# Moving the block quantizer of a second FFN from GpSimd and VectorE to VectorE alone

## The reference

```python
def fake_quant_nvfp4(x, global_scale):          # blocks of 16
    amax = max(abs(xb))                         # per block
    sc8 = clip(amax / 6 * global_scale, 0, 448).astype(float8_e4m3fn)
    dq = sc8 / global_scale
    a = clip(abs(xb) / dq, 0, 6)
    q = sign(xb) * nearest(a, [0, .5, 1, 1.5, 2, 3, 4, 6])
    return q * dq
gate, up = quant(x) @ quant(gate_w).T, quant(x) @ quant(up_w).T
return quant(silu(gate) * up) @ quant(down_w).T
x = x + ffn(layernorm(x))
```

## Time and profile before

| | |
|---|---|
| runs | 979.66, 979.79, 981.98 us |
| median | 979.79 us |
| span of the profiled execution | 977.3 us (the profiler gives no time of its own for it beside the span) |
| busy: PE, DVE, ACT, POOL | 614.2, 629.9, 342.3, 329.3 us |
| mean granted clock of TensorE | 0.784 of full speed |

### The profile page before, as it was taken

One profiled execution on the slowest core, in us unless ns is written; L12 is line 12 of the kernel. 1 busy time (PEld: TensorE's weight loads), 2 busy tenths in 40 slices (PEclk: granted clock), 3 DMA queues, 4 the chain that ended last, 5 costly groups with the idle time before them and its releaser, 6 DMA issues.

```text
span 977.3 us, 19947 instructions
## 1 busy us (share of the span) xinstructions
PE 614.2 (63%) x5798; PEld 435.2 (45%) x5804; DVE 629.9 (64%) x2044; ACT 342.3 (35%) x797; POOL 329.3 (34%) x560
## 2 busy tenths in 40 slices
PE   5699999878886899922122227999981276722331
PEld 3588888754444666601010015777750154511110
DVE  2576767637773788778888865666646523267774
ACT  2255555522221465521111112444430134422332
POOL 2112111145553222146656553222100123255441
PEclk9799999979996899965555556999995569955555
DMA  8422232200001344200000012322300135300001
GB/s 247 93 64 58 60 71 56 50 8 1 0 0 33 90 98 97 66 9 0 0 0 0 0 26 64 82 70 64 73 15 0 33 107 136 105 1 0 0 0 43
DMA packets 99780, 46.96 MB, mean 48 GB/s; under 512 B 82992, under 2 KB 92272, under 8 KB 99696
## 3 DMA queue, kind: packets, MB, share of 16 engines
q1 hardware_dynamic: 99728, 46.34, 19.3%
HBM read 26.39 MB, written 19.92 MB: 47 GB/s over the span
## 4 chain that ended last, share of the span: by engine, by line
PE 36%; issue 22%; DVE 13%; POOLq 11%; POOL 10%; DVEq 4%; ACT 2%; DMA 1%; SPq 0%; ACTq 0%
PE bank L463 3%; POOL stats L994 3%; PE bank L430 2%; PE bank L492 2%; PE bank L435 2%; PE bank L446 2%; PE bank L414 2%; POOLq L1050 2%; POOLq L1052 2%; POOL small L1072 2%; PE bank L424 2%; POOLq L1055 2%; POOL att_t L1059 2%; PE bank L565 2%; PE bank L487 1%
## 5 line engine op out<-in xcount | busy, mean ns | idle before, releaser
L994 POOL TENSOR_TENSOR stats<-stats,half_neg 128x1 f32<-128x1 f32 x112 | 63.3, 565 | 251.1 <-DVE stats L1283 243.8
L808 ACT ACTIVATE probs<-bank 128x512 f32<-128x512 f32 x160 | 95.2, 597 | 88.3 <-PE bank L435 87.6
L1310 DVE TENSOR_REDUCE mx<-bank 128x4 f32<-128x512 f32 x160 | 108.1, 680 | 9.7 <-PE bank L414 9.1
L430 PE MATMUL bank<-q_stack,k_stack 128*128 128x128 bf16 x512 | 72.6, 222 | 1.5 <-DVE shift_t L1344 1.4
L435 PE MATMUL bank<-shift_t,sel_bf 128*128 128x128 bf16 x512 | 72.2, 221 | 0.0
L657 PE MATMUL bank<-ident_bf,probs 128*128 128x128 bf16 x16 | 4.6, 286 | 105.5 <-POOL probs L1053 105.5
L1021 POOL CAST q_parts<-resid 128x128 bf16<-128x128 f32 x48 | 14.4, 300 | 149.5 <-DVE resid L1325 149.5
L1288 DVE TENSOR_SCALAR xn<-x_sb,stats 128x128 f32 (+1 forms) x96 | 37.3, 389 | 35.4 <-POOL stats L994 35.1
L1325 DVE SCALAR_TENSOR_TENSOR resid<-bank,w_bias_cols,q_parts 128x128 f32<-128x128 f32 x48 | 16.8, 350 | 64.6 <-ACT q_parts L854 63.9
L1294 DVE TENSOR_TENSOR x_sb<-bank,x_sb 128x128 f32 (+1 forms) x64 | 18.5, 289 | 61.9 <-PE bank L570 26.6
L430 PEld LDWEIGHTS bank<-q_stack,k_stack 128*128 128x128 bf16 x512 | 50.1, 99 | 7.4 <-issue 5.8
(11 more groups left out here) (272 smaller groups left out, 1845.5 us busy)
## 6 DMA issues: line engine op xcount, KB each, us to landing
k_stack<-scratch_k SPq DMA_DIRECT2D x48, 192.0 KB, 3.4
q_stack<-scratch_q SPq DMA_DIRECT2D x48, 192.0 KB, 3.2
scratch_k<-k_parts SPq DMA_DIRECT2D x48, 96.0 KB, 1.8
scratch_q<-q_parts SPq DMA_DIRECT2D x48, 96.0 KB, 1.8
scratch_k<-k_parts SPq DMA_DIRECT2D x48, 64.0 KB, 1.6
scratch_q<-q_parts SPq DMA_DIRECT2D x48, 64.0 KB, 1.8
scratch_k<-k_parts SPq DMA_DIRECT2D x48, 32.0 KB, 1.5
scratch_q<-q_parts SPq DMA_DIRECT2D x48, 32.0 KB, 1.6
```

The source lines that it names most:

```text
L430: last = mm(o, k_stack[:, s, h, :], q_stack[:, s, h, :], start=layer == 1, stop=False, skip_group_check=True)
L808: activation(probs[:, (sP * U + u) % 4, :], bank[2 + u % 2][:, :], ACT.Tanh if layer == 3 else ACT.Exp, scale=float(d) ** -0.5).then_inc(s ...
L994: tt(stats[:, s, 9:10], stats[:, s, 8:9], half_neg[:, :], ALU.pow).then_inc(ln_rstd, 1)
L1310: reduce(mx[:, sM, u * UNIT:(u + 1) * UNIT], bank[u % 2][:, :].rearrange("p (h k) -> p h k", h=UNIT), AX.X, ALU.max).then_inc(sm["mx"], 1)
```

## The change

The wide instructions that GpSimd had in this FFN are removed there and a new function `fp4_blocks` does the whole quantization on VectorE, in the same step that computes the block scales. The order within it: product with the reciprocal scales; exponent mask, taken from the upper 16 bits of each 32-bit word (`[:, 1::2]` of a 16-bit view) into a 16-bit tile `magic4`; max and multiply on that 16-bit tile; then lower clip and addition of the magic number in one three-operand instruction, subtraction, and upper clip and product with the scale in another one. VectorE's waits for `pw` go, its semaphores `e` and `hf` too, and the wait for attention 1's last value product moves from GpSimd's step 1 to VectorE's step 0. `hh` is now raised at the end of VectorE's step k for what GpSimd's step k + 1 did before. Blank lines of the diff are left out.

```diff
--- before.py
+++ after.py
@@ -14,6 +14,7 @@
 F32 = mybir.dt.float32
 BF16 = mybir.dt.bfloat16
 U8 = mybir.dt.uint8
+U16 = mybir.dt.uint16
 U32 = mybir.dt.uint32
 ALU = mybir.AluOpType
 ACT = mybir.ActivationFunctionType
@@ -174,7 +175,7 @@
         dst4 = probs[:, :, :].rearrange("p s w -> p (s w)").bitcast(BF16)[:, 0:SLOTS * W4]
         dst4 = dst4.rearrange("p (s w) -> p s w", s=SLOTS)
         work4 = att_t[:, :, :].rearrange("p s w -> p (s w)")
-        a4, b4 = work4[:, 0:W4], work4[:, W4:2 * W4]
+        a4, magic4 = work4[:, 0:W4], work4[:, W4:2 * W4].bitcast(BF16)[:, 0:W4]
         small4 = small[:, :, :, :].rearrange("p s i n -> p s (i n)")
         GROUP = 4
@@ -1040,24 +1041,6 @@
                     s0, s1 = k % SLOTS, (k - 1) % SLOTS
                     if on(k, 0):
                         rstd(3, t, k)
-                    if k == 1:
-                        pool.wait_ge(S[1]["av"], 4 * B)
-                    if 1 <= k < B + 3:
-                        cols, _, n, (_, sc, _, _) = live4(k - 1, s1)
-                        a_, b_ = a4[:, cols], b4[:, cols]
-                        pool.wait_ge(f["hf"], t)
-                        tt(a_, a_, b_, ALU.add)
-                        pool.drain()
-                        tt(a_, a_, b_, ALU.subtract)
-                        pool.drain()
-                        tt(blocks(dst4[:, s1, cols], n), blocks(a_, n), per_block(sc, n), ALU.mult
-                           ).then_inc(f["hh"], 1)
-                        pool.drain()
-                    if k < B + 2:
-                        cols, _, n, (_, _, _, rs) = live4(k, s0)
-                        pool.wait_ge(f["e"], t + 1)
-                        tt(blocks(a4[:, cols], n), blocks(src4[:, k % 2, cols], n), per_block(rs, n), ALU.mult
-                           ).then_inc(f["pw"], 1)
                 return step
             def ffn0_step():
@@ -1171,6 +1154,21 @@
                 ts(b_.bitcast(U32), a_.bitcast(U32), EXPONENT, None, ALU.bitwise_and)
                 drain()
                 return ts(b_, b_, 1.0, FP4_MAGIC, ALU.max, ALU.mult)
+            def fp4_blocks(src, dst, work, magic, n, sc, rs):
+                tt(blocks(work, n), blocks(src, n), per_block(rs, n), ALU.mult)
+                drain()
+                ts(magic.bitcast(U16), work.bitcast(U16)[:, 1::2], EXPONENT >> 16, None, ALU.bitwise_and)
+                drain()
+                ts(magic, magic, 1.0, FP4_MAGIC, ALU.max, ALU.mult)
+                drain()
+                stt(work, work, -FP4_MAX, magic, ALU.max, ALU.add)
+                drain()
+                tt(work, work, magic, ALU.subtract)
+                drain()
+                return stt(blocks(dst, n), blocks(work, n), FP4_MAX, per_block(sc, n), ALU.min, ALU.mult)
             def quantize8(src, dst, scale, work=(tmp_a, tmp_b)):
@@ -1451,10 +1449,6 @@
                                    ALU.mult)
                     if on(k, 0):
                         ln_stats(3, t, k)
-                    if 1 <= k < B + 3:
-                        dve.wait_ge(f["pw"], t)
-                        cols = live4(k - 1, s1)[0]
-                        binades(a4[:, cols], b4[:, cols]).then_inc(f["hf"], 1)
                     if on(k, 2):
                         ub = bank[3 + 2 * (s2 % 2)]
                         dve.wait_ge(f["sg"], t - 1)
@@ -1466,7 +1460,12 @@
                     if k < B + 2:
                         drain()
                         cols, bs, n, tiles = live4(k, s0)
-                        block_scales(src[:, cols], n, tiles, gs[:, bs], gs_up[:, bs]).then_inc(f["e"], 1)
+                        block_scales(src[:, cols], n, tiles, gs[:, bs], gs_up[:, bs])
+                        drain()
+                        if k == 0:
+                            dve.wait_ge(S[1]["av"], 4 * B)
+                        fp4_blocks(src[:, cols], dst4[:, s0, cols], a4[:, cols], magic4[:, cols], n, tiles[1], tiles[3]
+                                   ).then_inc(f["hh"], 1)
                     if on(k, 4):
                         held(dve, "dve", f["o_ps"], t - 3)
                         residual(t - 4, bank[7][:, 128:256], s4, w_scale[:, 7:8])
```

## The result

| | before | after |
|---|---|---|
| first comparison, median | 979.81 us | 986.84 us, ratio 1.0068 [1.0045, 1.0091] |
| second comparison, median | 980.82 us | 987.09 us, ratio 1.0051 [1.0025, 1.0078] |
| span of the profiled execution | 977.3 us | 982.9 us |
| busy: DVE, POOL | 629.9, 329.3 us | 641.1, 236.4 us |

The change makes the kernel slower by 6 to 7 us. GpSimd lost 93 us of busy time and VectorE gained 11: what VectorE won by GpSimd's silence is less than the work it took over.

The account below looks back on a forecast made before the run. VectorE's serial list was taken to bound the second FFN. Loop +6.2, ramp +7.4 and tail -6.7 summed to +6.9 us, time 986.7 us; the 8-in-10 range ran from 981.5 to 994.

Parts of the forecast that it names:

- Bound: Second FFN: VectorE's serial list of instructions sets the loop step's period, 9.64 us before the change.
- Excesses, 2.17 a step: Loop step: three VectorE instructions stretched beside GpSimd's wide ones return to short times, saving 2.17 us.
- Root's wait, 0.82 from L1281 to L1286: Loop step: with the clips gone, VectorE's normalization waits for GpSimd's reciprocal root, 0.82 us where 2.53 stood.
- The stall of 0.08: Loop step: VectorE's wait for the reciprocal root that comes out from under the removed clips, 0.08 us.
- Two-input instructions, 0.826 at 640 columns: Added quantizer on VectorE: four instructions with two tensor inputs, 0.826 us each at 640 columns, 3.30 together.
- Mask 0.49, 16-bit max and multiply 0.33: Added quantizer on VectorE: strided 16-bit mask 0.49 us, max and multiply with 16 bits on both sides 0.33.
- Added list, 4.52: Loop step: six new instructions and drains take 4.52 us from the reciprocal scales to the residual, where 0.12 stood.
- Step +0.52: Loop: each of twelve steps grows from 9.64 to 10.16 us, +6.2 us in all.
- Ramp +7.4: Steps 0 to 3: +3.9 us for steps 0 and 1 together, +3.3 for step 2, +0.2 for step 3.
- Tail -6.7: Steps 16 to 19 with two early next-attention steps: 26.8 us against 33.57, as the quantizer finishes one step earlier.
- The rival that the next attention gives the gain back: After the stage: waiting for the next attention's stack load returns half to all, 990 to 993 us; chance 0.08.
- The wait for attention 1's last product: VectorE's step 0: product ends at 418.60 us, VectorE gets there at about 420.9, so the wait costs nothing.

Follow-up runs that it names:

- narrow_pool: The kernel before the change, with GpSimd's three rounding instructions done on the first block of 16 columns alone; 951.18 us.
- clips: The changed kernel with both clips in an instruction of their own and plain two-tensor instructions for the add and last product; 1000.36 us.
- wide_pool: The changed kernel with three idle products of 640 columns per step (steps 2 to 15) put on GpSimd; 1015.65 us.
- late: The changed kernel with all of the quantizer still on VectorE but one step later; 992.60 us.
- two_pool: The changed kernel with the reciprocal-scale product and the subtraction on GpSimd, VectorE's step reordered around them; 963.37 us, ratio 0.9812 to the kernel before.

## Why the prediction was right

It said 986.7 us and +6.9; the medians are 986.84 and 987.09. By its steps:

- **Bound.** VectorE's list before and after: shown from both sides by narrow_pool (-2.16 a step) and clips (+0.58).
- **Excesses, 2.17 a step.** wide_pool brought back 2.00 on the same lines, narrow_pool took away 2.16.
- **Root's wait, 0.82 from L1281 to L1286.** Measured 461.01 - 460.19 = 0.82. The stall of 0.08 inside it was not seen as one: the view shows no wait there.
- **Two-input instructions, 0.826 at 640 columns.** 0.826 and 0.825. The scaling from 128 and 512 columns held, and the scalar clip in them is free.
- **Mask 0.49, 16-bit max and multiply 0.33.** 0.494 and 0.327. The first was the nearest row, the second the middle between two ends, so luck in part. For the second the Trainium skill's page "VectorE: DVE Perf Modes", section The perf-mode tier table, had led to an estimate of 0.32: the run agrees.
- **Added list, 4.52.** 4.50.
- **Step +0.52.** +0.49 in the mean. The single steps shown grew from 9.62 to 10.06 us, by 0.44: the added list is 0.02 short of the forecast, and the next statistics start 0.26 us after the residual instead of 0.33. The reason for this is open; it is not that GpSimd's waits are gone, for `late` has none and shows 0.33. The other 0.05 of the mean is idle time at the loop's turns.
- **Ramp +7.4.** +7.04. Steps 0 and 1 added 3.88 (3.9), step 2 3.28 (3.3). Step 3 lost 0.12 where I had added 0.2: the 0.23 at the loop's entry did not come again.
- **Tail -6.7.** -6.87; late shows its cause, +6.3 when the quantizer moves back a step. The rival that the next attention gives the gain back has fallen: what lies behind the stage is 0.07 us longer, not 3 to 7.
- **The wait for attention 1's last product** cost nothing: it ended at 418.1 us, VectorE reached its wait at 420.4, and no wait shows there.

The terms add up to +6.9 where the stage gave +6.03, and the profiled spans differ by 5.6. That the medians differ by 6.3 to 7.0 and so hit the forecast closely is partly chance: single runs of the kernel after fell anywhere in 982.6 to 991.0, and in the two profiled ones the difference lay in stages that the change does not touch. That the last transposes start 0.5 us before VectorE's last early instruction was an assumption without a row; the trace after shows 0.70, and 2.20 instead of 2.06 from there to the residual, so two small errors nearly cancelled.

## What to carry to other kernels

Work beside the bounding engine is not free and not lost: price it by what it stretches. Look for short instructions with long times, and put the helper's wide instructions beside ones with a PSUM input or beside reductions. Here the version that did so, with the clips fused, was 18 us faster, while taking the helper out cost 6. When a stage is one serial list, sum the list: instruction, drain, and what the new order does at ramp and tail, which can be as large as the loop's change and of the other sign.

## What was not expected of the hardware

- When one of the short instructions that are stretched here starts inside a wide one of GpSimd, it lasts until just behind the other's end: 0.18 became 1.08 us beside a product of 1.29. When it starts first, by as little as 0.01 us, it keeps its 0.18.
- GpSimd's subtraction with one 16-bit input took 1.40 us at 640 columns in two_pool, the one with two 32-bit inputs 1.53 in the kernel before.
- A mask over every second 16-bit word costs what it costs over all 32-bit words, 0.494 us at 640 columns.
